# Graph layer with two layer norms: bias rows spread by TensorE, reordered hops and loads at the start, one split taken later

## The reference, cut to what matters

```
u      = h h^T / sqrt(384);  p = softmax(u);  delta = p * adjacency
attn   = delta / (sum(delta, axis=2) + 1e-10)
h_left = h W_left^T + b_left   (h_self, h_right likewise)
ctx    = attn[j > i] h_left + diag(attn) * h_self + attn[j < i] h_right
o      = relu(layernorm(ctx, eps 1e-12) * gamma + beta)
out    = layernorm(x + o, eps 1e-5)
```

## Time and profile before

| what | us |
|---|---|
| median of 3 runs | 484.27 (484.2 to 484.92) |
| the profiled execution's own time | 482.74 |
| its span (first to last instruction) | 481.0 |
| PE busy | 455.7, 95% of the span |
| DVE, ACT, POOL busy | 360.1, 325.5, 224.6 |

### The profile page before, as it was taken

How to read it: one execution, slowest core, us unless ns; L and a number is a source line. 1 busy time by engine, 2 the same in 40 slices (tenths; PEclk the granted TensorE clock), 3 DMA queues, 4 the chain that set the end, 5 groups by cost and what they waited for, 6 DMA issues and landing times.

```text
span 481.0 us, 9617 instructions
## 1 busy us (share of the span) xinstructions
PE 455.7 (95%) x2709; PEld 453.1 (94%) x2709; DVE 360.1 (75%) x1082; ACT 325.5 (68%) x714; POOL 224.6 (47%) x297
## 2 busy tenths in 40 slices
PE   6973999999999999999999999999999999999992
PEld 6963999999999999999999999999999999999982
DVE  4645777887778888777778877778878777877756
ACT  5724666876676677667667766776777677667752
POOL 0404345455543445554444555444555544455552
PEclk9995999999999999999999999999999999999997
DMA  7654454555655555565545556564555556454221
GB/s 236 213 186 132 154 161 155 178 187 176 208 166 176 167 173 184 175 203 185 185 146 170 184 182 190 185 201 144 167 179 185 181 189 203 154 169 130 92 71 65
DMA packets 85634, 81.64 MB, mean 170 GB/s; under 512 B 7280, under 2 KB 77680, under 8 KB 85616
## 3 DMA queue, kind: packets, MB, share of 16 engines
q1 hardware_dynamic: 85616, 81.42, 53.7%
HBM read 52.56 MB, written 28.84 MB: 169 GB/s over the span
## 4 chain that ended last, share of the span: by engine, by line
PE 87%; DMA 3%; POOL 2%; ACT 2%; DVE 2%; issue 2%; SPq 1%; POOLq 0%; DVEq 0%; ACTq 0%
PE ps_proj L437 58%; PE ps_ctx L451 20%; PE ps_scores L425 4%; PE ps_scores L416 4%; DMA bias<-in_L_gnn_b_left 1%; DMA dt_dram<-turned 1%; POOL w_lo L926 1%; POOL rstd L940 1%; POOL shifted L948 0%; DMA dt_raw<-dt_dram 0%; ACT ps_proj L526 0%; DMA cross_dram<-cross_turned 0%; POOL scaled L944 0%; ACT normed L556 0%; ACT ps_scores L507 0%
## 5 line engine op out<-in xcount | busy, mean ns | idle before, releaser
L437 PE MATMUL ps_proj<-w_hi,xt_hi 128*128 128x384 f32 x576 | 195.0, 339 | 14.2 <-ACT ps_proj L526 14.2
L437 PE MATMUL ps_proj<-w_lo,xt_hi 128*128 128x384 f32 x576 | 194.4, 338 | 0.0
L437 PE MATMUL ps_proj<-w_hi,xt_lo 128*128 128x384 f32 x576 | 194.2, 337 | 0.0
L940 POOL TENSOR_TENSOR rstd<-var_eps,minus_half 128x4 f32<-128x4 f32 x32 | 42.5, 1329 | 190.3 <-DVE var_eps L741 187.8
L437 PEld LDWEIGHTS ps_proj<-w_hi,xt_hi 128*128 128x128 f32 x576 | 109.0, 189 | 15.4 <-ACT ps_proj L526 15.0
L437 PEld LDWEIGHTS ps_proj<-w_lo,xt_hi 128*128 128x128 f32 x576 | 108.9, 189 | 0.0
L437 PEld LDWEIGHTS ps_proj<-w_hi,xt_lo 128*128 128x128 f32 x576 | 108.8, 189 | 0.0
L530 ACT ACTIVATE proj_hi<-ps_proj 128x384 fp32r<-128x384 f32 x128 | 63.2, 496 | 53.7 <-PE ps_proj L437 53.7
L526 ACT ACTIVATE ps_proj<-bias 128x384 f32<-128x384 f32 (+1 forms) x192 | 92.6, 496 | 1.1 <-DMA bias<-in_L_gnn_b_left 1.0
L944 POOL TENSOR_TENSOR scaled<-normed,gamma_sb 128x384 f32<-128x384 f32 x62 | 63.2, 1019 | 40.2 <-ACT normed L556 40.2
L707 DVE TENSOR_TENSOR proj_lo<-ps_proj,proj_hi 128x384 fp32r<-128x384 f32 x128 | 69.3, 547 | 15.2 <-ACT proj_hi L530 14.7
(11 more groups left out here) (87 smaller groups left out, 658.5 us busy)
## 6 DMA issues: line engine op xcount, KB each, us to landing
x_sb<-in_x SPq DMA_DIRECT2D x32, 384.0 KB, 4.4
xt_sb<-in_x_t SPq DMA_DIRECT2D x31, 384.0 KB, 3.8
out_dram<-out_sb SPq DMA_DIRECT2D x31, 384.0 KB, 2.9
adj_sb<-in_adj SPq DMA_DIRECT2D x32, 256.0 KB, 4.5
cross_dram<-cross_turned SPq DMA_DIRECT2D x31, 256.0 KB, 2.1
cross_raw<-cross_dram SPq DMA_DIRECT2D x124, 64.0 KB, 2.0
dt_dram<-turned SPq DMA_DIRECT2D x31, 256.0 KB, 2.0
dt_raw<-dt_dram SPq DMA_DIRECT2D x124, 64.0 KB, 2.1
```

Of the source, the lines that this page charges most:

```text
L437: mm = nc.tensor.matmul(ps_proj[bank(at, g)][:, 0:H], stationary, moving[w][:, c, :], start=False, stop=True, skip_group_check=True)
L940: nc.gpsimd.tensor_tensor(rstd[at.slot(2)][:], var_eps[:], minus_half[:], ALU.pow).then_inc(rstd_ready, 1)
```

## The change

It touches four things at the start of the kernel and nothing in the loop of the later batches.

1. The left and right biases are no longer loaded 128 times by SP. ACT issues two transfers of one row each, after one small activation (first_read); PE multiplies a row of ones with each row (float32, 384 columns) into ps_ctx, the left one between the second and third chunk of the first scores, the right one behind them; DVE copies each result to SBUF. ps_ctx is therefore not opened with zeros at the beginning, but both halves of it after group 4 of batch 0.
2. SP, in the body of batch 0, issues the adjacency of batch 2 first, then both stores of the hops (cross(2), turned(1)), then both loads back, and only then x of batches 1 and 2.
3. The lo halves of the self weights are made by DVE in place of POOL, ahead of turn_cross(1), which itself now stands ahead of diagonal(0).
4. In batch 1 alone, ACT and DVE take split_delta later: ACT behind seed 4, DVE behind split_proj 1.

```diff
--- before.py
+++ after.py
@@ -117,6 +117,9 @@
         w_hi = [sb(f"w_hi{w}", [P, C, H], F32R) for w in range(3)]
         w_lo = [sb(f"w_lo{w}", [P, C, H], F32R) for w in range(3)]
         bias = [sb(f"bias{w}", [P, HE]) for w in range(3)]
+        bias_row = [sb(f"bias_row{w}", [1, H]) for w in (LEFT, RIGHT)]
+        ones_row = sb("ones_row", [1, P])
+        first_read = sb("first_read", [P, 1])
         gamma_sb = sb("gamma_sb", [P, H])
         beta_sb = sb("beta_sb", [P, H])
 
@@ -178,7 +181,11 @@
 
         first_xt_loaded = [sem(f"first_xt_loaded{c}") for c in range(C - 1)] + [xt_loaded[0]]
         w_loaded = [[sem(f"w_loaded{w}_{c}") for c in range(C)] for w in range(3)]
-        bias_loaded = [sem(f"bias_loaded{w}") for w in range(3)]
+        bias_row_loaded = [sem(f"bias_row_loaded{w}") for w in (LEFT, RIGHT)]
+        self_bias_loaded = sem("self_bias_loaded")
+        ones_row_ready = sem("ones_row_ready")
+        bias_spread = sem("bias_spread")
+        bias_ready = sem("bias_ready")
         vectors_loaded = sem("vectors_loaded")
         stored = [sem(f"stored{i}") for i in range(2)]
 
@@ -299,25 +306,19 @@
                                  ).then_inc(cross_loaded, 16)
 
             w_rows = [wt.rearrange("(c p) e -> p c e", p=P) for wt in (wt_left, wt_right, wt_self)]
-            biases = (b_left, b_right, b_self)
 
             def load_weight(w):
                 for c in range(C):
                     sp.dma_start(w_raw[w][:, c, :], w_rows[w][:, c, :]).then_inc(w_loaded[w][c], 16)
 
-            def load_bias(w):
-                sp.dma_start(bias[w][:, 0:H], biases[w].partition_broadcast(P)).then_inc(bias_loaded[w], 16)
-
             for c in range(C):
                 sp.dma_start(xt_sb[0][:, c, :], xt_rows[0][:, c, :]).then_inc(first_xt_loaded[c], 16)
             load_weight(LEFT)
-            load_bias(LEFT)
             sp.dma_start(adj_sb[0][:], adj_rows[0]).then_inc(adj_loaded[0], 16)
             load_weight(RIGHT)
-            load_bias(RIGHT)
             load_xt(1, 1)
             load_weight(SELF)
-            load_bias(SELF)
+            sp.dma_start(bias[SELF][:, 0:H], b_self.partition_broadcast(P)).then_inc(self_bias_loaded, 16)
             load_xt(2, 2)
             sp.dma_start(adj_sb[1][:], adj_rows[1]).then_inc(adj_loaded[1], 16)
             for to, vector in ((gamma_sb, gamma), (beta_sb, beta)):
@@ -340,9 +341,15 @@
                         sp.wait_ge(xt_lo_ready, at.n(1, C - 1))
                     load_xt(third.n(1), third.slot(UNROLL))
                 if at.b == 0:
+
+                    sp.dma_start(adj_sb[2][:], adj_rows[2]).then_inc(adj_loaded[2], 16)
                     store_cross(ahead)
+                    store_turned(nxt)
                     load_cross(ahead)
-                    sp.dma_start(x_sb[1][:], x_rows[1]).then_inc(x_loaded[1], 16)
+                    load_turned(nxt)
+                    for b in (1, 2):
+                        sp.dma_start(x_sb[b][:], x_rows[b]).then_inc(x_loaded[b], 16)
+                    return
                 if ahead.exists(BATCHES):
                     if at.plus(-2).exists(BATCHES):
 
@@ -350,11 +357,11 @@
                     load(ahead.n(1), ahead.slot(UNROLL))
                 if nxt.exists(BATCHES):
                     store_turned(nxt)
-                if ahead.exists(BATCHES) and at.b != 0:
+                if ahead.exists(BATCHES):
                     store_cross(ahead)
                 if nxt.exists(BATCHES):
                     load_turned(nxt)
-                if ahead.exists(BATCHES) and at.b != 0:
+                if ahead.exists(BATCHES):
                     load_cross(ahead)
 
             every_batch(sp, BATCHES, one)
@@ -378,6 +385,8 @@
 
             def first_scores(at):
                 for c in range(C):
+                    if c == C - 1:
+                        spread(LEFT)
                     pe.wait_ge(xt_lo_ready, c + 1)
                     for t in range(T):
                         hi, lo = xt(at, c, t * P, (t + 1) * P)
@@ -388,9 +397,15 @@
                                                   stop=(c == C - 1 and i == 2), skip_group_check=True)
                 mm.then_inc(scores_ready, 1)
 
+            def spread(w):
+
+                pe.wait_ge(bias_row_loaded[w], 16)
+                nc.tensor.matmul(ps_ctx[:, w, 0:H], ones_row[:], bias_row[w][:], start=True, stop=True).then_inc(bias_spread, 1)
+
             def first_turn(at):
 
                 pe.wait_ge(delta_ready, T)
+                pe.wait_ge(bias_ready, 2)
                 for t in range(T):
                     for h in range(T):
                         k = T * t + h
@@ -398,8 +413,10 @@
                 mm.then_inc(first_dt_ready, 1)
 
             def open_context(at):
+
                 pe.wait_ge(dt_lo_ready, 1)
-                nc.tensor.matmul(ps_ctx[:, 1, 0:HE], zeros[:, 0:P], zeros[:], start=True, stop=True).then_inc(ctx_opened, 1)
+                for t in range(T):
+                    nc.tensor.matmul(ps_ctx[:, t, 0:HE], zeros[:, 0:P], zeros[:], start=True, stop=True).then_inc(ctx_opened, 1)
 
             def keys(tile):
 
@@ -453,14 +470,16 @@
 
 
             pe.wait_ge(zeros_ready, 1)
-            for to in (*(p[:, 0:HE] for p in ps_proj), *(ps_ctx[:, t, 0:HE] for t in range(T))):
-                mm = nc.tensor.matmul(to, zeros[:, 0:P], zeros[:], start=True, stop=True)
+            for to in ps_proj:
+                mm = nc.tensor.matmul(to[:, 0:HE], zeros[:, 0:P], zeros[:], start=True, stop=True)
             mm.then_inc(banks_opened, 1)
             pe.wait_ge(ident_ready, 1)
             for _ in range(WARM_UP):
                 nc.tensor.transpose(ps_scores[1][:, 0, 0:P], ident[:], ident[:])
             first = Batch(0, 0)
+            pe.wait_ge(ones_row_ready, 1)
             first_scores(first)
+            spread(RIGHT)
 
             def one(at):
                 nxt, ahead = at.plus(1), at.plus(2)
@@ -474,10 +493,11 @@
                         first_turn(at)
                     if at.b == 0 and g == 3:
                         cross(nxt)
+                    if at.b == 0 and g == 4:
+                        open_context(at)
                     if g == 4 and at.b != 0 and ahead.exists(BATCHES):
                         cross(ahead)
                 if at.b == 0:
-                    open_context(at)
                     squares(nxt)
                     cross(ahead)
                 if not last(at):
@@ -511,14 +531,14 @@
             def seed_proj(at, g):
                 w, _ = GROUPS[g]
                 if at.b == 0 and g == PBANKS:
-                    act.wait_ge(bias_loaded[w], 16)
+                    act.wait_ge(self_bias_loaded, 16)
                 if g >= PBANKS:
 
                     act.wait_ge(proj_lo_ready, at.n(NSPLIT, g - PBANKS + 1))
                 elif at.b != 0 and g + 2 < NSPLIT:
                     act.wait_ge(proj_lo_ready, at.n(NSPLIT, g + 2 + 1 - NSPLIT))
                 elif at.b == 0:
-                    act.wait_ge(bias_loaded[w], 16)
+                    act.wait_ge(bias_ready, w + 1)
                 else:
 
                     act.wait_ge(ctx_seeded, at.n(T, g + 2 + 1 - NSPLIT - T))
@@ -545,8 +565,8 @@
                 act.wait_ge(proj_ready, at.n(NG, order(at).index(NSPLIT + t) + 1))
                 if t == 0:
                     act.wait_ge(diag_ready, at.n(T, T))
-                if t == 1 and at.b == 0:
-                    act.wait_ge(ctx_opened, 1)
+                if t == 0 and at.b == 0:
+                    act.wait_ge(ctx_opened, T)
                 nc.scalar.activation(ps_ctx[:, t, 0:HE], ps_proj[bank(at, NSPLIT + t)][:, 0:HE], ACT.Copy,
                                      scale=diag[at.slot(2)][:, t:t + 1]).then_inc(ctx_seeded, 1)
 
@@ -568,6 +588,11 @@
                                          ).then_inc(out_ready, 1)
 
             first = Batch(0, 0)
+
+            act.wait_ge(zeros_ready, 1)
+            nc.scalar.activation(first_read[:], zeros[:, 0:1].bitcast(F32), ACT.Copy)
+            for w, vector in ((LEFT, b_left), (RIGHT, b_right)):
+                act.dma_start(bias_row[w][:], vector.partition_broadcast(1)).then_inc(bias_row_loaded[w], 16)
             split_first_xt()
             for c in range(C):
                 split_weight(LEFT, c)
@@ -607,13 +632,16 @@
                 if at.b == 0:
 
                     return
-                split_delta(at)
+                if at.b != 1:
+                    split_delta(at)
                 split_proj(at, 0)
                 normalise(before)
                 split_proj(at, 1)
                 if nxt.exists(BATCHES):
                     exps(nxt)
                 seed_proj(at, 4)
+                if at.b == 1:
+                    split_delta(at)
                 split_proj(at, 2)
                 seed_proj(at, 5)
                 if last(at):
@@ -764,12 +792,17 @@
                 for t in range(T):
```

(15 more changed lines are left out.)

## The result

The median of 20 runs is 479.3 us (477.75 to 482.81), against 483.08 (481.02 to 485.2) for 20 runs of the kernel before taken with them. The ratio is 0.9927 [0.9911, 0.9943]: faster by 0.7%, some 3.5 us where 12.3 were forecast, and 479.3 lies above the range, which ended at 476.3. The profiled execution after took 482.81 us, before 482.74, so the two profiles show no gain at all. (Of the 20 executions after it is the slowest; the one before is near its median.) The question is where 12 us went.

What follows compares the result with a forecast made beforehand. PE was taken to bound the loop, so time gained at the start moves the end. Terms -1.3 - 9.6 + 0.4 - 2.1 + 0.3 = -12.3 us took 484.27 to 472.0 (profiled 482.74 to 470.4); range 469.8 to 476.3.

Steps and rivals of the forecast that it cites:

- Step 1: Biases at the start: spreads at 0.26 us each inside PE's first wait, first projection near 8.75, 1.0 us sooner.
- My clock paragraph: After group 4 of batch 1: a 1.3 us wait leaves the clock full, matmuls run at 0.162 us, 2.1 us less.
- Step 2: Self weights on DVE: turn_cross(1) at about 16.3, squares(2) at about 24.6, -1.3 us.
- Step 3: SP's order in batch 0: wait ahead of group 4 of batch 1 about 1.3 us instead of 10.9, -9.6 us.
- Step 4: Later split_delta(1): deltas(2) end near 34.8, but cross(3) behind group 4 wants them at 34.5, +0.4 us.
- Batch 2's +0.3: Ahead of group 4 of batch 2: PE there at 47.7, released at 47.9 after the hop, +0.3 us.
- The term of -2.1 for the clock: Group 4 of batch 1 and what follows: 18 matmuls at full clock instead of 4.99 us, -2.1 us.
- The loop is left alone: Later batches: PE bounds the loop, the change leaves it alone, and a batch stays at 13.96 us.
- A: Hops of cross(2) or dt(1) land late: wait 4.3 us, perhaps low clock, 475 to 476 us; chance 0.22.
- B: First scores: bias row lands late at 8.0, PE near 10.6 instead of 8.75, 473.9 us; chance 0.13.
- D: Every batch: PE waits behind the hops in a closed circle, kernel slower, 495 us at 0.8 over; chance 0.03.

Runs made afterwards that it cites:

- the first experiment: The changed kernel run again with no edit, against the kernel before: 478.97 us, ratio 0.9905.
- the four places mended: Changed kernel with 128-row spreads, turn_cross(3) ahead of the first residual, early adjacency of batch 2, new tiles last: 472.88 us, 0.9784 of the kernel before.

## Why the prediction was wrong

**The wait went as forecast.** From 10.91 it came down by 9.0, where 9.6 was forecast. The path of 2.6 us from finish_scores to group 4, and the 7.3 from squares(2) to the end of group 3, held to 0.1. Full clock after the wait held in this profile, and that was luck: of eleven profiles with a wait of 1.8 to 2.0 there, six kept it.

**Step 1 failed first, in the price of the spreads and in its clock.** I took 0.26 us for each spread, with 0.53 as the upper bound, by transposes. One takes 7.21 - 6.37 = 0.84. Transposes of 128 columns gave no upper bound for this product. By the four passes of the Trainium skill ("FP8 and Floating Point Precision", TensorE Precision Notes) it was 0.7 by estimate, and the trace sides with that: 0.84 here, and 9.41 - 8.71 = 0.70 with 128 rows. I called both spreads covered by PE's wait, and they were: the start at 8.95 is 0.2 off. What the sum left out is the clock. Eleven matmuls at 0.32 instead of 0.18 us cost 1.6 us. My clock paragraph looked at waits alone, and PE had none here. With 128 rows in the same product the low clock is gone, in four profiles of four, where one row had it in five of eight. So it is likely, not shown beyond doubt, that how many rows a matmul reads matters, and not only that PE is busy.

**Step 2's -1.3 became +1.5.** Group 2 was 1.7 later than forecast, hence turn_cross(1) at 18.28 instead of 16.3. (The 16.3 was also 0.2 too early: cross(1) ended at 16.62 + 0.87 = 17.49 before, and 1.0 less is 16.5.) The first hop then took 0.8 longer than before (18.28 to 25.99, against 17.59 to 24.47). Why is open. A packet of q8 falls into this hop in every profile, before the change too (21.59). The load of adjacency(2) close behind it can be a part: with that load early the hop took 7.2 to 7.4 in four profiles, with SP's old order 6.71, and with the change's order 7.5 to 8.0 in seven, but 6.90 in one. Together that makes 27.48 instead of 24.6. The gain on the diagonals came as forecast (0.25 and 0.28), but lay where PE was not waiting for it.

**Step 3 was right in mechanism and 0.7 short.** From squares(2) to the release of group 4 were to pass 8.5 us, and 9.2 did. I forgot norm_shift, which stands ahead of finish_scores on DVE and waits for POOL: 0.7 us, all of it, by the experiment that moved it. What I credited to part 2 alone is shared with part 4, as undoing either shows. **Step 4's +0.4** was no wait in the end: cross(3) starts at 38.38 right behind group 4.

**Batch 2's +0.3 was the largest miss.** From squares(3) to squares(4) 67.54 - 12.3 - 40.4 = 14.8 us were forecast, and 64.16 - 44.08 = 20.1 passed. I had turn_cross(3) done 6.3 us after group 4 began; it took 7.3, since the residual ahead of it waited 1.23 for POOL and then took 1.36. I gave the store the 2 us of quiet ones; it took 4.4, with an instruction fetch in its middle. That the fetch is the cause is argued, not tested. That made a wait of 2.83, 2.5 more than forecast, and behind it 21 matmuls took 6.17 us where 21 x 0.162 = 3.4 were to be had: 2.8 of clock. The term of -2.1 for the clock was thus won in batch 1 and paid again in batch 2.

**"The loop is left alone" was false.** No instruction of it changed, but the tiles behind the new ones moved, by 4 bytes more than a multiple of 512: 3.3 us, by the two kernels that undo it. This is a term that the sum put at nothing.

The ledger for the profiled executions: 2.9 at squares(2), 0.7 at group 4, 5.2 in batch 2 and 3.3 in the loop are 12.1 of the 12.4 by which 482.81 exceeds the forecast of 470.4. Where no low clock follows batch 2's wait, 2.8 of it don't arise, as in the first experiment. The ledger is thus that of the slowest execution; the medians are 479.3 - 472.0 = 7.3 apart. With the four places mended the profiled execution is 472.67, 2.3 from the forecast. Of the rivals, A named the place (waits move to the hops, with low clock) but the wrong batch and size; B and D did not happen, since the rows landed in time and PE doesn't wait in the loop.

## What to carry to other kernels

A wait that is removed is worth only what no wait further on takes back, so follow the next two batches with their queues as closely as the first. When PE bounds the loop, compare its matmuls per microsecond before and after, even if the loop's code is untouched: a new small tile can move its operands, and small tiles are best allocated last. Work that fills a wait on PE is not free if it is narrow: watch the granted clock behind it.

## What the runs showed of the hardware

- **Narrow float32 products and the clock.** Five profiled kernels with spreads of one row had the clock up and then half, 1.2 GHz, as the first projection began, with PE never idle; the four with 128 rows, and the two without spreads, kept it. Three others with one row differ: one rose only at 15.0, and two did not fall. With so few profiles that is likely an effect of the one row, not certain.
- **Short waits and the clock.** A wait of 1.8 to 2.0 us at group 4 of batch 1 was followed by half clock in five profiles and not in six; in batch 2, 2.68 and 2.72 left it full, and 2.73 and 2.83 did not. So the length alone doesn't decide, and that 2.92 us had once left the clock full, as I argued from the earlier trace rows, is no rule. The Trainium skill ("TensorE: Matmul & The Clock Gate", What's actually happening) says that the monitor runs free of the kernel's start; the trace agrees in that the clock first rises between 4.8 and 8.0 us in thirteen profiles and at 15.0 in one.
- **Addresses.** float32r projections start every 0.1757 us instead of 0.1735 when the tiles behind the new ones lie 4 bytes further on. Seven profiles have the tiles moved by 4 bytes more than a multiple of 512 and 14.08 us per batch; seven have them at their old place, or moved by a multiple of 512, and 13.96; none is between.
- **Instruction fetches.** One packet of 16 KB on q8 in the middle of cross(3)'s store of 256 KB went with a landing after 3.4 to 4.6 us, in eight profiles. Stores of this size without one and without other traffic need 2.0; but turned(2)'s, at 39.35, with no packet of q8 and with loads beside it (up to 413 GB/s), took 3.8. Where cross(3)'s store came out earlier (40.77), the packet fell into loads instead, and four issues took 2.69 instead of 1.74. Before the change it fell at 52.4, into the loads. No run moved the fetch alone.
